# The last batch's gate chain in the Mix phase cut into two halves of the batch, with eight filling products fewer

## The reference, cut to what matters

```python
x = L0_attn_a_x                                              # 8 batches x 512 tokens x 256 channels
x = x + attention(layernorm(x))                              # phase 1
x = x + ffn(layernorm(x))                                    # phase 2: 8 experts, 2 for each token
x = x + mix(x)                                               # phase 3: two residual blocks, ends with x of phase 4
x = x + ffn(layernorm(x))                                    # phase 4: the same experts again

def ffn(h):                                                  # h: 4096 x 256
    scores = softmax(h @ gate_w.T)                           # 8 logits for each token
    top_scores, sel = top_k(scores, 2)
    order = argsort(sel.T.reshape(-1), stable=True)          # (token, choice) pairs sorted by expert
    y = grouped_swiglu(h[tok_sorted], counts, w1, w2, w3)
    return zeros.at[tok_sorted].add(y * scores_sorted)
```

## Time and profile before

| what | value |
|---|---|
| median of 3 runs | 1412.31 us (1410.61 to 1412.87) |
| the profiled execution: its own time / its span | 1410.74 us / 1409.0 us |
| mean granted TensorE clock over the span | 0.968 of full speed |
| PE busy / DVE / ACT / POOL, share of the span | 95% / 64% / 49% / 45% |
| the last batch's gate chain and the sorting, in the span | from about 1026 us to 1048 us |
| phase 4 (second pass over the experts), in the span | 1048 us to the end |

### The profile page before, as it was taken

One profiled execution on the slowest core, in us unless ns is written; L12 is line 12 of the kernel. 1 busy time (PEld: TensorE's weight loads), 2 busy tenths in 40 slices (PEclk: granted clock), 3 DMA queues, 4 the chain that ended last, 5 costly groups with the idle time before them and its releaser, 6 DMA issues. The chain is left out here.

```text
span 1409.0 us, 27926 instructions
## 1 busy us (share of the span) xinstructions
PE 1337.1 (95%) x7613; PEld 1128.8 (80%) x7614; DVE 902.7 (64%) x2172; ACT 684.2 (49%) x1543; POOL 628.2 (45%) x583
## 2 busy tenths in 40 slices
PE   6999998899999999976999999998979999999997
PEld 4999987788888888833787778777868888888886
DVE  5777889444444444458988898887864444444443
ACT  4576756233333333355587668766643333333332
POOL 4767663355555555424222222222223555555553
PEclk9999997899999999988999999999989999999999
DMA  8575854566665333370000000000327666633332
GB/s 277 210 269 195 292 218 136 181 163 160 160 164 110 57 57 56 46 227 0 1 16 31 0 30 30 30 1 31 121 65 216 160 164 166 162 71 56 57 53 42
DMA packets 100873, 157.84 MB, mean 112 GB/s; under 512 B 10256, under 2 KB 60688, under 8 KB 100816
## 3 DMA queue, kind: packets, MB, share of 16 engines
q1 hardware_dynamic: 73120, 118.67, 24.7%
q0 software_dynamic: 27264, 37.82, 16.7%
q10 hardware_dynamic: 432, 0.66, 0.2%
HBM read 95.89 MB, written 61.21 MB: 111 GB/s over the span
## 5 line engine op out<-in xcount | busy, mean ns | idle before, releaser
L1428 POOL DMA_INDIRECT out_x<-second_y,second_add_token x71 | 112.6, 1586 | 153.1 <-DMA out_x<-second_y,second_add_token 104.9
L1428 POOL DMA_INDIRECT x_rows<-first_y,first_add_token x70 | 111.2, 1589 | 148.0 <-DMA x_rows<-first_y,first_add_token 114.8
L1419 POOL DMA_INDIRECT xs<-normed_rows,gather_token x140 | 138.4, 989 | 44.9 <-issue 40.3
L1523 DVE TENSOR_TENSOR first_hT_lo<-bank,first_hT_hi 128x512 fp32r<-128x512 f32 x71 | 49.1, 692 | 160.0 <-ACT first_hT_hi L1456 160.0
L1523 DVE TENSOR_TENSOR second_hT_lo<-bank,second_hT_hi 128x512 fp32r<-128x512 f32 x71 | 49.1, 692 | 157.8 <-ACT second_hT_hi L1456 157.8
L172 PE MATMUL bank<-ring,first_xT_hi 128*128 (+1 forms) x284 | 118.7, 418 | 0.1
L172 PE MATMUL bank<-ring,second_xT_hi 128*128 (+1 forms) x284 | 118.7, 418 | 0.1
L174 PE MATMUL bank<-ring,second_xT_lo 128*128 (+1 forms) x284 | 112.7, 397 | 0.0
L174 PE MATMUL bank<-ring,first_xT_lo 128*128 (+1 forms) x284 | 112.5, 396 | 0.0
L173 PE MATMUL bank<-ring,second_xT_hi 128*128 (+1 forms) x284 | 112.4, 396 | 0.0
L173 PE MATMUL bank<-ring,first_xT_hi 128*128 (+1 forms) x284 | 112.2, 395 | 0.0
(11 more groups left out here) (472 smaller groups left out, 3903.8 us busy)
## 6 DMA issues: line engine op xcount, KB each, us to landing
ring<-split_weights SPq DMA_DIRECT2D x192, 256.0 KB, 3.0
a_wraw<-in_L_ffn_w SPq DMA_DIRECT2D x21, 512.0 KB, 6.4
split_weights<-a_whi SPq DMA_DIRECT2D x21, 512.0 KB, 2.6
split_weights<-a_wlo SPq DMA_DIRECT2D x21, 512.0 KB, 3.5
normed_rows<-xg SPq DMA_DIRECT2D x16, 528.0 KB, 3.3
x_rows<-x SPq DMA_DIRECT2D x8, 512.0 KB, 7.1
x<-x_rows SPq DMA_DIRECT2D x8, 512.0 KB, 6.0
out_x<-x SPq DMA_DIRECT2D x8, 512.0 KB, 3.2
```

Of the source, the lines that this page charges most:

```text
L1419: nc.gpsimd.indirect_dma_start(xs[q][:], None, normed_dram[:], bass.IndirectOffsetOnAxis(ap=gather_token[q][:], axis=0)).then_inc(loaded[q ...
L1428: nc.gpsimd.indirect_dma_start(x_dram[:], bass.IndirectOffsetOnAxis(ap=add_token[q][:], axis=0), y[q], None, compute_op=ALU.add).then_inc( ...
L1523: nc.vector.tensor_tensor(hT_lo[par][:].rearrange("p k t -> p (k t)"), th_bank[par][:], hT_hi[par][:].rearrange("p k t -> p (k t)").bitcas ...
```

## The change

Statistics, scales, normalisation, transposes, copies and gate products of the last batch are each done for tiles 0 and 1 and then for tiles 2 and 3. On ACT the first half of the normalisation stands between `send_tokens` 4 and `send_tokens` 5, and `send_tokens` 6 stands behind the copy of the logits. On PE the eight fillers ahead of the transposes are four, and the four between transposes and products are gone.

```diff
...
+            def route_norm_half(h):
+                act.wait_ge(rstdg_ready, B + h)
+                act.sem_inc(passed["act"], 1)
+                for j in range(2 * h, 2 * h + 2):
+                    last = nc.scalar.activation(xg[:, j, 0:C], tile_of(x, B - 1, j), ACT.Identity, bias=shiftg[:, j:j + 1],
+                                                scale=mvg[:, j, 1:2])
+                last.then_inc(xg_ready, 1)
...
-            for n in range(4, EARLY):
-                send_tokens(nc, act, route, const, n)
-            route_norm(B - 1)
-            gate_rows(B - 1)
+            send_tokens(nc, act, route, const, 4)
+            act.wait_ge(rows_stored, 16 * (B - 1))
+            route_norm_half(0)
+            send_tokens(nc, act, route, const, 5)
+            route_norm_half(1)
+            for h in range(2):
+                act.wait_ge(t_filled, round_gate(B - 1) + 1 + 2 * h)
+                for i in range(KC):
+                    last = nc.scalar.activation(xgT[:, i, h * C:(h + 1) * C], tbk[i][:, h * C:(h + 1) * C], ACT.Copy)
+                last.then_inc(t_emptied, 1)
+            act.wait_ge(t_filled, round_gate(B - 1) + 4)
+            nc.scalar.activation(lg[:], tbk[0][:, 0:TB * EX].rearrange("p (t e) -> p t e", e=EX), ACT.Copy).then_inc(t_emptied, 1)
             send_tokens(nc, act, route, const, EARLY)
-            gate_logits(B - 1)
             row_exp(B - 1)
...
-            rstd(mvg, shiftg, own_c, varg_ready, rstdg_ready, B - 1)
+            for h in range(2):
+                rstd(mvg, shiftg, own_c, varg_ready, rstdg_ready, B - 1 + h, 2 * h, 2 * h + 2)
...
             for j in range(2):
-                nc.vector.bn_stats(bng[:, j, :], tile_of(x, B - 1, j))
+                last = nc.vector.bn_stats(bng[:, j, :], tile_of(x, B - 1, j))
+            placing.link(last, passed["dve"])
+            for j in range(2):
+                last = nc.vector.bn_aggr(mvg[:, j, :], bng[:, j, :])
+            last.then_inc(varg_ready, 1)
...
-            for j in range(TB):
+            for j in range(2, TB):
                 last = nc.vector.bn_aggr(mvg[:, j, :], bng[:, j, :])
...
             count_choices(nc, pe, route, const, 1)
             pe.wait_ge(varg_ready, B)
-            keep_busy(nc, xb_[4][:], fk_hi[:, 0, 0:P], fk_hi[:, 0, 0:N], 8)
-            gate_transposes(B - 1)
             keep_busy(nc, xb_[4][:], fk_hi[:, 0, 0:P], fk_hi[:, 0, 0:N], 4)
-            gate_products(B - 1)
+            for h in range(2):
+                pe.wait_ge(xg_ready, B + h)
+                pe.wait_ge(t_emptied, round_gate(B - 1) + h)
+                for i in range(KC):
+                    for j in range(2 * h, 2 * h + 2):
+                        last = nc.tensor.transpose(tbk[i][:, j * P:(j + 1) * P], xg[:, j, i * P:(i + 1) * P], ident[:])
+                last.then_inc(t_filled, 1)
+                pe.wait_ge(t_emptied, round_gate(B - 1) + 1 + h)
+                for j in range(2 * h, 2 * h + 2):
+                    for i in range(KC):
+                        last = nc.tensor.matmul(tbk[0][:, j * EX:(j + 1) * EX], xgT[:, i, j * P:(j + 1) * P], gate_s[:, i, :],
+                                                start=(i == 0), stop=(i == KC - 1))
+                last.then_inc(t_filled, 1)
             place_tokens(nc, pe, route, EARLY)
```

More of the change, by code:

```diff
@@ L1998, in _, with rstd @@
         def _(pool):
-            def rstd(mvt, shiftt, own, ready, done, b):
+            def rstd(mvt, shiftt, own, ready, done, b, lo=0, hi=TB):
                 wait_apart(pool, ready, b + 1, passed["pool"])
-                nc.gpsimd.tensor_scalar(mvt[:, :, 0], mvt[:, :, 0], -1.0, None, ALU.mult)
-                nc.gpsimd.tensor_scalar(mvt[:, :, 1], mvt[:, :, 1], EPS, None, ALU.add).then_inc(own, 1)
+                mean, var = mvt[:, lo:hi, 0], mvt[:, lo:hi, 1]
+                nc.gpsimd.tensor_scalar(mean, mean, -1.0, None, ALU.mult)
+                nc.gpsimd.tensor_scalar(var, var, EPS, None, ALU.add).then_inc(own, 1)
                 pool.wait_ge(own, 2 * b + 1)
-                nc.gpsimd.tensor_tensor(mvt[:, :, 1], mvt[:, :, 1], neg_half[:, 0:TB], ALU.pow).then_inc(own, 1)
+                nc.gpsimd.tensor_tensor(var, var, neg_half[:, lo:hi], ALU.pow).then_inc(own, 1)
                 pool.wait_ge(own, 2 * b + 2)
-                nc.gpsimd.tensor_tensor(shiftt[:], mvt[:, :, 0], mvt[:, :, 1], ALU.mult).then_inc(done, 1)
+                nc.gpsimd.tensor_tensor(shiftt[:, lo:hi], mean, var, ALU.mult).then_inc(done, 1)
             def rstd_in(b):
@@ L2226, in softmax_begin @@
                 s_.round(b)
-                wait_apart(dve, t_emptied, round_gate(b) + 2, passed["dve"])
+                wait_apart(dve, t_emptied, round_gate(b) + (3 if static(b, B - 1) else 2), passed["dve"])
                 top_experts(nc, s_, lg, tp, ti, passed, top_ready)
```

## The result

The changed kernel takes 1415.33 us (median of 13 runs, 1413.04 to 1416.41) against 1410.58 us for the kernel before in the same rounds: ratio 1.0029, 95% interval 1.0022 to 1.0036, so 3.1 to 5.1 us slower. Predicted were 1417.5 on 1412.31, a ratio of 1.0037.

A forecast was written before the change was run, and what follows sets the result against it. It took the start of the last batch's logits copy, which leads to phase 4's first gather, as the bound: 4.75 later, plus 0.1 and 0.3, makes 5.15 on 1412.31, so 1417.5 us; range 1412.6 to 1419.4.

The forecast's parts named there:

- the rivals with another clock: Gate chain on PE: clock lost then back, 1415.7 us, chance 0.18; clock kept throughout, 1414.2 us, chance 0.17.
- the store that does not bind: Rival: ACT sees batch 6's rows stored by 1027.8, so no wait; 1412.6 us, no difference; chance 0.12.
- the upper bound 1419.4: Top of the likeliest case's range, with products at 1.0 to 1.7, tail 0 to 1.1, phase 4's start -0.7 to +0.7.
- the first rival: Clock falls, but four fillers restore 1.00 before the first gate products; logits 3.2 later, 1415.7 us; chance 0.18.
- Statistics and scales cost nothing: DVE and POOL: the early half's aggregate and steps fit in DVE's 0.66 us idle time, nothing on the path.
- The store's landing ends last, and send 5 stands behind it: ACT: batch 6's store lands at 1029.4, ACT stands 1.7 us after send 4, send 5 waits until 1030.5.
- Group 5's placing late, fillers on the path, transposes at 10.2: PE: group 5 placed about 1032.4 instead of 1029.82, then count and four fillers; transposes at 1034.7 at half clock.
- The halves in series: PE's gate chain: each half waits for ACT's copy, no overlap; 4.8 us for both at full clock, before 4.26.
- Which clock: PE: granted clock falls between 1030 and 1033 and stays at 0.50 for the whole gate chain; chance 0.50.
- my 4.75: Logits of the last batch at 1041.4 against 1036.64 before, 4.75 us later, with the chain at half clock.
- A half of the chain at half clock 3.35: Gate chain, one half at clock 0.50: transposes 0.95, products 1.6, 3.35 us in all; 6.7 for both.
- Behind the logits: From logits to gather: send 6 ahead of the choice's copy adds 0.1, last placing and fillers 0.3 (0 to 1.1).

The follow-up runs named there:

- x3: The changed kernel with the last batch's normalised rows in a buffer of their own, so no wait for batch 6's store; ratio 1.0006 to the kernel before.
- x1: The changed kernel with ACT's send of group 5 put back ahead of the wait for the stored rows; ratio 0.9996 to the kernel before.
- x2: The changed kernel with nine more fillers on PE between the placing of groups 4 and 5; ratio 1.0010 to the kernel before.
- x8: The changed kernel without its four fillers ahead of the transposes; ratio 1.0032 to the kernel before.
- x6: The kernel before with four fillers ahead of the transposes instead of eight and none between transposes and products; ratio 1.0022 to the kernel before.
- x9: The changed kernel with nine fillers between placing groups 4 and 5, and both halves' transposes ahead of both halves' products; ratio 1.0005 to the kernel before.
- x7: The changed kernel with send 5 ahead of the store wait and both halves' transposes ahead of both halves' products; ratio 0.9996 to the kernel before.
- x10: The same kernel as x7, run once more; ratio 0.9999 to the kernel before.

## Why the prediction was right, and where its path was not

The time lay inside the range, and the direction and the mechanism were those named first; the size was 3.1 to 5.1 us for 5.15. The range, 1412.6 to 1419.4, also held the rivals with another clock and, at its lower end, the store that does not bind, so lying in it says little: the traces decide. Two figures do not come out of their own terms: the upper bound 1419.4 is 1419.2 (5.15 + 0.2 + 0.8 + 0.7 on 1412.31), and the first rival's 1415.7 is 1415.8. Step by step:

- *Statistics and scales cost nothing*: right; 0.28 of DVE's idle time was left.
- *The store's landing ends last, and send 5 stands behind it*: right. The trace names the DMA, and the first half starts at 5.02 from the mark (predicted 1029.5 - 1024.48 = 5.02). x3 and x1 show it from both sides: with no wait, or with nothing behind it, the loss is gone.
- *Group 5's placing late, fillers on the path, transposes at 10.2*: right, 10.21; the placing ended at 8.17, predicted 7.9.
- *The halves in series*: right as a mechanism. With the clock kept (x2) the chain from the transposes to the logits takes 4.74 (predicted 4.8; before, 4.26).
- *Which clock*: the step that failed. "Four fillers and four transposes look like that stretch, not like nine fillers": they did bring the clock back, within 1037 to 1038, as the first rival said. But the rival was not right to the end either: the clock fell again in the second products, 1.47 for 1.06. Hence 3.66 at the logits, between the rival's 3.2 and my 4.75. x8 shows that it was the fillers: without them the clock stayed at 0.50.
- *A half of the chain at half clock 3.35*: too small. The products took 1.87 a half in x8 for 1.6, and 3.58 for 16 in x6 against 1.95 at full. The transposes took 1.1 for 0.95: the row behind that figure, 1.74 for eight from 228.98, ran at 0.50 only in its first four fifths; within 230.00 to 230.50 the clock was 0.65 in the mean, and 1.00 behind. The rows below are the weight loads of the gate products in x1, at full clock, and in x8. The rule of the Trainium skill ("TensorE: Matmul & The Clock Gate", section on LDWEIGHTS), which names no clock and by which the products would cost the same at either level, disagrees with these rows: a load took 192 ns at 1.00 and 333 at 0.50.

```profile
L2565 PEld LDWEIGHTS bank<-gate,b_xgT x16: 186/192/193, 1033.7 to 1036.8; 128*128 128x128 f32 x16
L2564 PEld LDWEIGHTS bank<-gate,b_xgT x16: 285/333/333, 1035.3 to 1040.3; 128*128 128x128 f32 x16
```

- *Luck in the size*: x8's chain at half clock takes 7.34 from the transposes to the logits, where 6.7 was predicted. Had the clock stayed at 0.50 as predicted, the logits would have come at 10.21 + 7.34 = 17.55, 5.39 later than before and not 4.75 (an estimate from these rows). The term that was too small hid a part of the clock's error.
- *Behind the logits*: ACT's copy of the choice came 0.17 later behind the logits than before (predicted 0.1), and the two fillers behind the last placing took 1.03 for 0.68; the gather came 4.00 later in all (predicted 5.15). From the mark this pair of executions ends only 3.44 apart, since 0.77 went again between the gather and phase 4's first product of line 172: 5.39 before, where the first gather's transfer took 3.68, and 4.62 after; from there to the end it was 0.21 more. In the other twelve executions, two of them of the old order, this stretch is 4.58 to 4.71, so it is the one profile of the kernel before that has a late transfer there. Why that transfer was late is not shown.

The loss has one cause, the wait in the middle of ACT's list, and three prices, which do not add up: the late placing, the serial halves behind it, and the clock. Mend the order (x1) or the wait (x3), and the loss is gone from the time; x9 leaves the wait and makes up for most of it by what PE does in the hole and behind it.

## What to carry to other kernels

When a chain is cut into pieces to start early, look at which wait the first piece now meets that used to be over in time, and at what stands behind it in the same queue: here a buffer's store, and a send that another engine needed at once. Two halves in series make the chain itself longer (4.74 for 4.26 in x1) and gain only what the early start gives; with the second half's work in the first half's waits it got shorter (3.33 in x7), and that took other PSUM banks and another order. A hole on PE costs its length and can cost the clock too, so price it at both levels, and fill it where it is, not where the old one was.

## What the runs showed of the hardware that was not expected

- The 128x8 gate products slow down nearly with the clock: 16 in 1.95 at granted 1.00, 3.58 at 0.50; the weight load of one is 192 ns of a product's 256 at full and 333 of 361 at half.
- In x6 a hole of 1.34 us behind four fillers was followed by the fall of the clock, within the microsecond in which the hole ended; before, behind eight fillers, the hole was 0.41, and the clock was kept.
- Two executions of one kernel (x7 and x10) with the same logits to 0.01 us differed by 1.16 at the gather: the last group's eight products ran at 0.50 in one and at 1.00 in the other, and the fillers behind them too.
